# A vision and text block on one Trainium2 core: the expert down projection in split halves by columns, with its weights multiplied in by GpSimd

## The chip, the core and the metric

The kernel runs on one core of a Trainium2 chip. Its engines are TensorE (PE in the profile, with its weight loads as PEld), VectorE (DVE), ScalarE (ACT), GpSimd (POOL) and SyncE (SP); each has its own instruction queue, and they meet through semaphores. The metric is the time of one launch on the device, in microseconds.

## The reference

32 images become 196 patch rows each, a class row is put ahead and 128 text rows behind, so each of the 32 batch elements is a matrix of 325 tokens x 192. On it run one causal attention block (12 heads of 16) and one feed-forward block, each behind a layer norm and with a residual. The part that changes is the feed-forward block:

```python
shared_out = _expert(x, shared_gate, shared_up, shared_down)      # silu(x@gate) * (x@up) @ down, 192 -> 384 -> 192
routing_probs = sigmoid(x @ router_w + routing_bias)              # 3 experts
scores, indices = top_k(routing_probs, 2)
scores = scores / scores.sum(axis=-1, keepdims=True)
combine_w = (one_hot(indices, E) * scores[..., None]).sum(axis=-2)
h = silu(einsum('bsh,ehi->ebsi', x, routed_gate)) * einsum('bsh,ehi->ebsi', x, routed_up)
out_e = einsum('ebsi,eih->ebsh', h, routed_down)
return shared_out + einsum('ebsh,bse->bsh', out_e, combine_w)
```

All is float32. Where speed matters the kernel writes a number as a high part rounded to float32r (a format in which TensorE takes one pass) and a low part, the rest, and multiplies high by high, high by low and low by high.

## The kernel before

The program is a software pipeline over the batch elements, one **turn** per element, 32 in all; each engine runs `turn(i, at, N, D, T, L, A, F)`. In turn i the feed-forward part is that of element b3 = i - 1, scores, softmax and values those of b2 = i, and the first norm and the q, k, v projections those of b1 = i + 1. N is the number of patch tiles embedded in the turn: 2 in 12 turns, 1 in 16, 0 in the last four. A and L say whether there still is an element b2 or b1. A token matrix has three tiles of 128, 128 and 70 columns, so `COLS` is 326.

A turn has two halves on TensorE. In the **unit half** it alternates twelve `unit(k)` (gate and up products of 128 of the 4 x 384 inner columns, three units an expert, the shared one first) with twelve `score(k)`. ACT makes `tanh` of each unit and `exp` of each score, DVE makes the activation `ht[:, k]` of it (`gate`, `up`), and GpSimd multiplies the exponentials by the causal mask: `mask_last` and `mask_full` for each of the six head pairs p, behind exponentials 2p + 1 and 2p + 2. In the **second half** come `value(g)` for three groups of two pairs, each behind the masks of its pairs, then transpositions, projections, the second norm, the query and key transpositions, the router, and between them the down projections.

```python
def value(g, b, F):
    ...
    pe.wait_ge(masked.sem, masked.at(b, 4 * g + 4))
```

`down(e, t, b)` has the tokens of tile t as the stationary operand and `w_down_s` as the moving one, in plain float32, so its result lies by token rows. There is one accumulation for each of four experts and three tiles, of three products each: 36 products of 192 columns a turn. DVE's `sum_up(n)` adds them into `o` one expert at a time, the routed ones scaled by the routing weight of the row. That weight (`route[:, 6]`) is made by `route_turn` on TensorE (three 128 x 128 transpositions of `route_e`), `route_sum` and `route_pick` on DVE, in the second half of the turn.

GpSimd also makes the inverse root of each norm (`inverse_root`, four small instructions one behind the other). The first norm's comes behind the masks of pair 1, and ACT needs it ahead of its first `scaled` instruction, which stands behind exponential 6 (k = 6 of its loop, counted from 0). The order on each engine is the order of the code. SP's queue issues in a turn: the copy `residual<-h`, four loads of the next element, the doublings of q and k (each `DMA` of `double_q` and `double_k`), the store of embedded rows, and the two stores of `out`. Of these the doublings for element i are issued while TensorE is already in the unit half of turn i.

## Time and profile before

| | |
|---|---|
| three runs | 1615.01, 1617.93, 1619.52 us; median 1617.93 |
| span of the profiled execution | 1613.5 us (no other time of that execution is given) |
| PE / PEld busy | 98% / 91% of the span |
| DVE / ACT / POOL busy | 73% / 55% / 25% |
| mean granted TensorE clock | 0.995 |

Busy shares are averages over unlike stretches. A turn without a stall at its ends can be followed in the timeline: the turn that the rows below are taken from begins its unit 0 at 911.60 us and the next one at 960.19 us.

### The profile page before, as it was taken

To read this page: it belongs to the slowest core of one execution; us is meant where nothing else is said; L and a number is where in the kernel's file an instruction comes from. 1 tells how busy PE (TensorE), PEld (TensorE's weight loads), DVE (VectorE), ACT (ScalarE), POOL (GpSimd) and SP (SyncE) were. 2 spreads that over 40 slices of the span, in tenths; PEclk is the share of its full clock that TensorE was granted. 3 is DMA by queue.
4 is the path that set the end of the run, shared out by engine and by line. 5 is a ranking of instruction groups with operands and counts; after the bars stand their busy time and mean duration, and the time that the engine had idled before them with its cause. 6 is when DMAs were issued, how large, how long until landed. Compare 5 with 4: busy or idle time off the path is not lost.

```text
span 1613.5 us, 46379 instructions
## 1 busy us (share of the span) xinstructions
PE 1575.5 (98%) x16536; PEld 1471.0 (91%) x16536; DVE 1182.2 (73%) x3383; ACT 880.0 (55%) x1896; POOL 409.1 (25%) x647
## 2 busy tenths in 40 slices
PE   6899999999999999999999999999999999999999
PEld 6699999999999999999999999999999999998988
DVE  6776777767777777777677777677777677777665
ACT  4555554556545565545565555566555566555552
POOL 0332321232321323212323212323212323212320
PEclk8999999999999999999999999999999999999999
DMA  6211221111211112201111111111111111110110
GB/s 217 76 37 58 69 69 38 47 60 62 69 49 45 52 59 69 69 34 47 45 49 57 55 37 38 47 49 57 55 38 38 46 49 57 51 39 32 37 33 13
DMA packets 75382, 86.80 MB, mean 54 GB/s; under 512 B 12721, under 2 KB 64329, under 8 KB 75209
## 3 DMA queue, kind: packets, MB, share of 16 engines
q1 hardware_dynamic: 64776, 65.45, 11.9%
q10 hardware_dynamic: 10560, 20.74, 3.9%
q8 instruction: 29, 0.48, 0.1%
q14 instruction: 17, 0.13, 0.0%
HBM read 32.44 MB, written 12.51 MB: 28 GB/s over the span
## 4 chain that ended last, share of the span: by engine, by line
PE 86%; DVE 5%; DMA 5%; SPq 1%; issue 1%; ACT 1%; POOL 0%; DVEq 0%
PE ps L426 79%; PE ps L429 6%; DMA kt<-kt 5%; DVE kt L1174 1%; DVE o L1071 1%; PE ps L626 1%; DVE rotated L1162 1%; SPq L368 1%; DVE qk_split L1167 1%; DVE xt L1102 1%; DMA router_bias<-in_b_router 0%; DVE stats L1091 0%; ACT wf L809 0%; DVE rotated L1134 0%; DVE h L1195 0%
## 5 line engine op out<-in xcount | busy, mean ns | idle before, releaser
L426 PE MATMUL ps<-xt,wf 64*128 64x326 f32 x6912 | 593.0, 316 | 0.0
L426 PEld LDWEIGHTS ps<-xt,wf 64*128 64x128 f32 x6912 | 523.0, 186 | 11.3 <-ACT qt L809 5.8
L426 PE MATMUL ps<-w_down_s,ht 128*128 128x192 f32 (+1 forms) x2304 | 413.9, 329 | 0.0
L426 PEld LDWEIGHTS ps<-w_down_s,ht 128*128 128x128 f32 (+1 forms) x2304 | 350.9, 174 | 14.3 <-issue 0.2
L1048 DVE SCALAR_TENSOR_TENSOR gated<-tanh_g,ps 128x326 f32<-128x326 f32 x384 | 189.1, 492 | 198.9 <-ACT tanh_g L823 198.9
L816 ACT ACTIVATE rows<-h,rstd 128x192 f32<-128x192 f32 (+2 forms) x279 | 151.1, 564 | 211.4 <-POOL rstd L1018 206.6
L1007 POOL TENSOR_TENSOR probs<-probs,causal 128x512 f32<-128x512 f32 x192 | 228.7, 1191 | 131.8 <-ACT probs L834 131.8
L834 ACT ACTIVATE probs<-ps 128x792 f32<-128x792 f32 (+1 forms) x384 | 254.3, 663 | 13.6 <-PE ps L426 13.2
L823 ACT ACTIVATE tanh_g<-ps 128x326 f32<-128x326 f32 x384 | 170.1, 443 | 164.1 <-PE ps L426 162.6
L1001 POOL TENSOR_TENSOR probs<-probs,causal 69x140 f32<-69x140 f32 x192 | 89.0, 464 | 473.8 <-ACT probs L834 473.7
L1054 DVE TENSOR_TENSOR ht<-gated,ps 128x326 f32<-128x326 f32 x384 | 190.1, 495 | 13.1
L426 PE MATMUL ps<-wa_hi,xt 128*128 128x288 f32 (+3 forms) x576 | 161.3, 299 | 2.6 <-DVE xt L1102 2.6
L1012 POOL TENSOR_TENSOR rstd<-mean_var,power 128x3 f32<-128x3 f32 x64 | 12.4, 194 | 545.6 <-DVE mean_var L1096 545.6
L426 PE MATMUL ps<-qt,kt 64*128 64x326 f32 (+2 forms) x1152 | 121.3, 258 | 11.9 <-DMA kt<-kt 11.3
L809 ACT ACTIVATE xt<-ps 128x326 fp32r<-128x326 f32 x224 | 84.4, 440 | 77.7 <-PE ps L429 77.7
L426 PE MATMUL ps<-wb,xt 128*128 128x288 f32 (+3 forms) x576 | 119.4, 289 | 0.0
L426 PEld LDWEIGHTS ps<-qt,kt 64*128 64x128 f32 (+1 forms) x1152 | 91.8, 168 | 21.6 <-DMA kt<-kt 15.9
L426 PE MATMUL ps<-probs,v_ones 128*32 128x198 f32 (+2 forms) x2304 | 109.8, 333 | 1.3
L1071 DVE SCALAR_TENSOR_TENSOR o<-ps,route,o 128x192 f32<-128x192 f32 (+1 forms) x288 | 104.3, 407 | 8.7 <-PE ps L426 7.8
L426 PEld LDWEIGHTS ps<-wa_hi,xt 128*128 128x128 f32 (+1 forms) x576 | 101.4, 176 | 7.4 <-ACT xt L809 1.4
L426 PEld LDWEIGHTS ps<-probs,v_ones 128*32 128x32 f32 (+1 forms) x2304 | 68.1, 109 | 42.3 <-issue 5.9
L1102 DVE TENSOR_TENSOR xt<-ps,xt 128x326 fp32r<-128x326 f32 x224 | 100.8, 486 | 6.4 <-ACT xt L809 6.4
(105 smaller groups left out, 1917.5 us busy)
## 6 DMA issues: line engine op xcount, KB each, us to landing
kt<-kt SPq DMA_DIRECT2D x384, 40.8 KB, 1.8
x_s<-in_xp ACTq DMA_DIRECT2D x40, 384.0 KB, 3.1
qt<-qt SPq DMA_DIRECT2D x132, 81.5 KB, 1.9
residual<-h SPq DMA_DIRECT2D x31, 288.0 KB, 2.4
out<-o SPq DMA_DIRECT2D x32, 192.0 KB
qt<-qt ACTq DMA_DIRECT2D x60, 81.5 KB, 2.0
kept_rows<-embed_rows SPq DMA_DIRECT2D x44, 96.0 KB, 1.7
h<-kept_rows SPq DMA_DIRECT2D x30, 95.2 KB
```

Of the source, the lines that this page charges most:

```text
L426: return nc.tensor.matmul(dst, lhs, rhs, start=first, stop=last)
L429: return nc.tensor.transpose(dst, src, ident[0:n, 0:n])
L809: return nc.scalar.activation(dst, src, ACT.Copy)
L816: return nc.scalar.activation(dst, src, ACT.Identity, bias=coef[:, 3, t:t + 1], scale=coef[:, 0, t:t + 1])
L823: nc.scalar.activation(tanh_g[:, k % 2, :], ps[:, GATE[k % 3], 0:COLS], ACT.Tanh, scale=0.5).then_inc(tanh_done.sem, 1)
L834: nc.scalar.activation(dst, src, ACT.Exp, scale=ATTN_SCALE / ROOT_GAIN ** 2).then_inc(exp_done.sem, 1)
L1001: nc.gpsimd.tensor_tensor(d, d, shaped(causal[0:REAL2], [[0, 2], [1, COLS2]]), ALU.mult).then_inc(masked.sem, 1)
L1007: nc.gpsimd.tensor_tensor(d, d, shaped(causal[:], [[0, 2], [0, 2], [1, P]]), ALU.mult).then_inc(masked.sem, 1)
L1048: v.scalar_tensor_tensor(out=gated[:, k % 2, :], in0=tanh_g[:, k % 2, :], scalar=1.0, in1=ps[:, GATE[k % 3], 0:COLS], op0=ALU.add, op1=ALU ...
L1054: v.tensor_tensor(ht[:, k, :], gated[:, k % 2, :], ps[:, UP[k % 3], 0:COLS], ALU.mult).then_inc(h_ready.sem, 1)
L1071: last = v.scalar_tensor_tensor(out=o[0:c, t, :], in0=d, scalar=route[0:c, 6, t, e - 1:e], in1=o[0:c, t, :], op0=ALU.mult, op1=ALU.add)
L1102: v.tensor_tensor(dst, ps[:, bank, 0:COLS], f32(hi), ALU.subtract).then_inc(low.sem, 1)
```

## The change

The down projection is turned round. The weights become the stationary operand and the 326 token columns the moving one; both are split into high and low parts in float32r, and all four experts are summed in one PSUM accumulation. The routing weight, which was applied behind the product, must then be multiplied onto the activations ahead of it.

- **Products.** `down_main(units)` has three products of 326 columns for each of twelve units (output columns 0 to 127); `down_rest(units)` has two, since 64 output columns of the high and 64 of the low weights stand side by side. They are 60 products a turn, spread over the second half. `out_turn` makes six transpositions back to rows, and DVE's `sum_out` adds the result to `o`, which a DMA has filled with `h1`.
- **Routing.** `route_turn` is three small products instead of transpositions, behind unit 0; `route_sum` and `route_pick` follow on DVE behind `up(0)` and `up(1)`. SP stores the weights to DRAM (`kept_weights`, one element of 4 bytes at a time, 1152 of them) and loads them back spread over the partitions (`weight_cols`, 3 x 326 on each of 128).
- **Splitting.** GpSimd's `weigh(k)` multiplies the nine routed units; ACT's `round_h` copies each of twelve units to `h_high`; the low part is the difference, `low_h`: units 0 to 2 on DVE, 3 to 11 on GpSimd.
- **Moved.** The first norm's `inverse_root` goes from behind pair 1 to behind pair 2, its moments on DVE from behind unit 1 to behind unit 2. `norm1_turn` goes ahead of `y_to_rows`, and `y_to_cols` uses PSUM banks 6 and 7. ACT takes three `round_h` between `keep_y(1)` and `keep_y(2)`. The `out` stores of an element go to the next turn of SP, ahead of the new DMAs.
- **Storage.** `h_high` and `qk_split` lie under `probs`, `h_low` under `ht`, `w_down_lo` under the raw weights. In the last turn (A false) DVE makes all twelve low parts.

The core of the diff; its three `turn` functions are those of SP, GpSimd and TensorE (second half), in this order:

```diff
+            def store_out(b):
+                sp.wait_ge(summed.sem, summed.at(b, SUMS))
+                sp.dma_start(out[b, 0:2 * P, :].rearrange("(t p) d -> p t d", p=P), o[:, 0:2, :]).then_inc(stored.sem, 16)
+                sp.dma_start(out[b, 2 * P:TOKENS, :], o[0:REAL2, 2, :]).then_inc(stored.sem, 16)
+                sp.wait_ge(stored.sem, stored.at(b, 32))
+            def spread_weights(b):
+                sp.wait_ge(pick_chain.sem, pick_chain.at(b, 7))
+                sp.dma_start(weight_rows, route[:, 6].rearrange("p t e -> p (t e)"), allow_slow_non_contiguous=True).then_inc(weights_stored.sem, 16)
+                if later(b):
+                    sp.wait_ge(h_weighted.sem, h_weighted.at(b - 1, ROUTED))
+                sp.wait_ge(weights_stored.sem, weights_stored.at(b, 16))
+                sp.dma_start(weight_cols[:], weight_spread).then_inc(weights_loaded.sem, 16)
             def turn(i, at, N, D, T, L, A, F):
+                sp.wait_ge(h1_ready.sem, h1_ready.at(b3, 1))
+                if later(b3):
+                    store_out(b3 - 1)
+                sp.dma_start(o[:], h1[:]).then_inc(o_copied.sem, 16)
+                spread_weights(b3)
...
+            def down_main(units, b, A):
+                for k in units:
+                    wait_low(k, b, A)
+                    acc = ps[:, DOWN_BANK, 0:COLS]
+                    mm(acc, w_down_hi[:, k, :], h_low[:, k, :], k == 0, False)
+                    mm(acc, w_down_lo[:, k, :], h_high[:, k, :], False, False)
+                    last = mm(acc, w_down_hi[:, k, :], h_high[:, k, :], False, k == UNITS - 1)
+            def down_rest(units, b, A):
+                for k in units:
+                    wait_low(k, b, A)
+                    w = w_down_rest[:, k].rearrange("p s c -> p (s c)")
+                    mm(ps[:, DOWN_BANK + 1, 0:COLS], w, h_low[:, k, :], k == 0, False)
+                    last = mm(ps[:, DOWN_BANK + 1, 0:COLS], w, h_high[:, k, :], False, k == UNITS - 1)
...
+            def weigh(units, b):
+                for k in units:
+                    if k == CHUNKS:
+                        pool.wait_ge(weights_loaded.sem, weights_loaded.at(b, 16))
+                    pool.wait_ge(h_ready.sem, h_ready.at(b, k + 1))
+                    nc.gpsimd.tensor_tensor(ht[:, k, :], ht[:, k, :], weight_cols[:, k // CHUNKS - 1, :],
+                                            ALU.mult).then_inc(h_weighted.sem, 1)
             def turn(i, at, N, D, T, L, A, F):
                 for p in range(PAIRS):
                     if A:
                         mask_last(p, i)
                         mask_full(p, i)
-                    if L and p == 1:
+                    if L and p == 2:
                         inverse_root(i + 1, n1_moments, mean_var, rstd, n1_root, n1_ready)
+                    if p > 2:
+                        weigh(range(2 * p - 3, 2 * p - 1), i - 1)
+                weigh(range(2 * PAIRS - 3, UNITS), i - 1)
                 if A:
+                    for k in range(CHUNKS, UNITS):
+                        low_h(k, i - 1)
                     inverse_root(i, n2_moments, mean_var2, rstd2, n2_root, n2_ready)
...
             def turn(i, at, N, D, T, L, A, F):
                 if A:
                     for g in range(GROUPS):
                         value(g, b2, F)
+                if L:
+                    norm1_turn(b1, F)
                 if A:
-                    route_turn(b3)
-                    down(0, 0, b3)
                     y_to_rows(b2)
-                    if L:
-                        norm1_turn(b1, F)
-                    down(0, 1, b3)
...
+                down_main(range(0, 1), b3, A)
                 if L:
                     for t in range(TILES):
                         project_qkv(t, b1, A)
+                    pe.wait_ge(v_kept.sem, v_kept.at(b1, 1))
                 if A:
                     y_to_cols(b2, F)
+                down_main(range(1, 5), b3, A)
...
                     project_y(b2)
+                if N:
+                    embed(at, N)
+                down_main(range(5, 9), b3, A)
+                down_rest(range(0, 6), b3, A)
                 if A:
                     norm2_turn(b2)
+                down_main(range(9, UNITS), b3, A)
+                down_rest(range(6, UNITS), b3, A)
                 if L:
                     first_groups(b1)
                     for n in range(2, 2 * GROUPS):
                         qk_turn(n, b1, at, N)
+                out_turn(b3)
```

GpSimd in the unit half of a turn, from the third head pair on, before the change (`probs` rows are the masks, a pair of them for each head pair):

```order
L1001 TENSOR_TENSOR probs<-probs,causal 69x2x70
L1005 REGISTER_ALU
L1007 TENSOR_TENSOR probs<-probs,causal 128x2x2x128
L999 REGISTER_ALU
L1001 TENSOR_TENSOR probs<-probs,causal 69x2x70
L1005 REGISTER_ALU
L1007 TENSOR_TENSOR probs<-probs,causal 128x2x2x128
```

The same place after it, from the mask of the fourth head pair on, with what each instruction waits for:

```order
L1066 TENSOR_TENSOR probs<-probs,causal 69x2x70 [waits exp_done]
L1070 REGISTER_ALU
L1072 TENSOR_TENSOR probs<-probs,causal 128x2x2x128 [waits exp_done]
L1089 ISA
L1090 ISA [waits weights_loaded]
L1091 TENSOR_TENSOR ht<-ht,weight_cols 128x326 [waits h_ready]
L1090 REGISTER_ALU
L1091 TENSOR_TENSOR ht<-ht,weight_cols 128x326 [waits h_ready]
L1064 REGISTER_ALU
L1066 TENSOR_TENSOR probs<-probs,causal 69x2x70 [waits exp_done]
```

Two multiplications now stand between each two of the last pairs' masks, and the first of them waits for the loaded routing weights.

SP's queue at the end of a turn and the start of the next before the change:

```order
L348 DMA kept_rows<-embed_rows 128x192 [waits rows_added]
L398 DMA out<-o 128x2x192 [waits summed]
L400 DMA out<-o 69x192 [waits summed]
L307 UNCONDITIONAL_BRANCH
L307 ISA
L386 ISA [waits h1_ready]
L387 ISA [waits hidden_loaded]
L388 DMA residual<-h 128x576 [waits txt_loaded]
```

And after it, the start of a turn:

```order
L406 ISA [waits h1_ready]
L407 ISA [waits summed]
L407 DMA out<-o 128x2x192
L408 ISA
L408 DMA out<-o 69x192
L409 ISA
L425 DMA o<-h 128x576 [waits stored]
L413 ISA
L414 DMA kept_weights<-route 128x9x1 [waits pick_chain]
L416 ISA
L417 ISA [waits h_weighted]
L418 DMA weight_cols<-kept_weights 128x3x326 [waits weights_stored]
```

Behind the stores of `out` the queue now waits until they have landed, then copies `h1`, and only then sends the routing weights out and back.

## Rows read from the trace of the kernel before

**Rows 1.** The page, busy time by engine.
```profile
PE 1575.5 (98%) x16536; PEld 1471.0 (91%) x16536; DVE 1182.2 (73%) x3383; ACT 880.0 (55%) x1896; POOL 409.1 (25%) x647
```
**Rows 2.** Busy time in windows: from, to, width; PE, PEld, DVE, ACT, POOL; clock.
```profile
911.60:933.60 22.00, 21.20 (x304) 19.89 (x305) 14.21 (x35) 15.53 (x33) 11.24 (x16) 1.00 0.21 70
933.60:960.20 26.60, 26.60 (x212) 24.88 (x212) 21.84 (x71) 11.83 (x27) 1.47 (x4) 1.00 0.08 28
```
**Rows 3.** Timeline of TensorE in one turn: start, length, line, names, count.
```profile
911.60 1.62 PE L426 MATMUL ps<-xt,wf 64*128 64x326 f32 x18
913.98 0.45 PE L426 MATMUL ps<-qt,kt 64*128 64x326 f32 x4 [0.75 <-DMA kt<-kt]
...
931.31 3.48 PE L426 MATMUL ps<-probs,v_ones 128*32 128x326 f32 x72
...
939.63 0.37 PE L426 MATMUL ps<-wa_hi,xt 128*128 128x288 f32 x1
...
943.68 0.73 PE L429 MATMUL ps<-ident,y_wide 128*128 128x128 f32 x6
...
950.71 3.09 PE L426 MATMUL ps<-w_down_s,ht 128*128 128x192 f32 x18
953.64 1.00 PE L429 MATMUL ps<-ident,rows 128*128 128x128 f32 x9
```
**Rows 4.** Timeline of GpSimd in the same turn.
```profile
921.04 0.19 POOL L1012 TENSOR_TENSOR rstd<-mean_var,power 128x3 f32<-128x3 f32 x1
921.32 0.85 POOL L1014 TENSOR_TENSOR rstd<-rstd,power 128x3 f32<-128x3 f32 x1
...
922.52 0.20 POOL L1018 TENSOR_TENSOR rstd<-rstd,power 128x3 f32<-128x3 f32 x1
...
923.09 1.19 POOL L1007 TENSOR_TENSOR probs<-probs,causal 128x512 f32<-128x512 f32 x1
924.79 0.47 POOL L1001 TENSOR_TENSOR probs<-probs,causal 69x140 f32<-69x140 f32 x1 [0.51 <-ACT probs L834]
```
**Rows 5.** Timeline of ACT in the same turn.
```profile
924.60 0.55 ACT L816 ACTIVATE rows<-h,rstd 128x192 f32<-128x192 f32 x1
```
**Rows 6.** Timeline of SP's queue in the same turn: start and length of each issue.
```profile
919.15 0.59 SPq L369 DMA_DIRECT2D kt<-kt  x1
920.03 0.38 SPq L348 DMA_DIRECT2D kept_rows<-embed_rows  x1
920.70 0.42 SPq L398 DMA_DIRECT2D out<-o  x1
921.38 0.26 SPq L400 DMA_DIRECT2D out<-o  x1
```
**Rows 7.** Waits of SP's queue in the whole span: in all, times, longest.
```profile
SPq L98 <- DMA out<-o: 1.9, 1, 1.9
```
**Rows 8.** The page, DMA issues: KB each, median us from issue to landing.
```profile
x_s<-in_xp ACTq DMA_DIRECT2D x40, 384.0 KB, 3.1
...
residual<-h SPq DMA_DIRECT2D x31, 288.0 KB, 2.4
...
kept_rows<-embed_rows SPq DMA_DIRECT2D x44, 96.0 KB, 1.7
```
**Rows 9.** The page, DMA queue of SP: packets, MB, share of 16 engines' span.
```profile
q1 hardware_dynamic: 64776, 65.45, 11.9%
```
**Rows 10.** Timeline of all engines near the start, 66 to 77 us.
```profile
65.97 2.46 POOL L1014 TENSOR_TENSOR rstd<-rstd,power 128x3 f32<-128x3 f32 x1
65.98 2.62 DVE L1319 TENSOR_TENSOR wf<-ht,wf 128x1536 fp32r<-128x1536 f32 x2
...
70.38 1.85 PE L429 MATMUL ps<-ident,rows 128*128 128x128 f32 x9 [1.63 <-ACT rows L816]
```
**Rows 11.** Two windows behind that stall, columns as in Rows 2.
```profile
72.00:74.00 2.00, 1.17 (x9) 0.91 (x9) 1.49 (x4) 2.00 (x6) 0.00 (x0) 0.50 0.39 128
...
76.00:78.00 2.00, 2.00 (x18) 1.96 (x16) 0.57 (x1) 0.31 (x1) 0.00 (x0) 0.55 0.29 100
```

More of the change, by code:

```diff
@@ L100, in sb, with under @@
             return ctx.enter_context(nc.sbuf_tensor(name, shape, dt))
+        def under(name, shape, *others):
+            with nc.sbuf_tensor(name, shape, F32) as first:
+                pass
+            return first, *(sb(other, like, dt) for other, like, dt in others)
         def signal(name, per_batch):
@@ L659, in route_turn, with wait_low @@
                 last.then_inc(route_turned.sem, 1)
-            def down(e, t, b, L=True, A=True):
-                if t == 0 and e == 0:
-                    pe.wait_ge(h_ready.sem, h_ready.at(b, UNITS if A else UNITS - 2))
-                    if not later(b):
-                        pe.wait_ge(s_halve, 2)
-                for c in range(CHUNKS):
-                    last = mm(accumulator(e, t, L, A), ht[:, CHUNKS * e + c, tile_cols(t)], w_down_s[:, CHUNKS * e + c, :],
-                              c == 0, c == CHUNKS - 1)
-                if t:
-                    last.then_inc(down_done.sem, 1)
+            def wait_low(k, b, A):
+                if k < CHUNKS:
+                    pe.wait_ge(shared_low.sem, shared_low.at(b, k + 1))
+                else:
+                    pe.wait_ge(routed_low.sem, routed_low.at(b, k - CHUNKS + 1))
@@ new lines, in down_main @@
+            def down_main(units, b, A):
+                for k in units:
+                    if k == 0 and not later(b):
+                        pe.wait_ge(s_down_low, 2)
+                    wait_low(k, b, A)
[3 more added lines that the diff above has]
+                    last = mm(acc, w_down_hi[:, k, :], h_high[:, k, :], False, k == UNITS - 1)
+                    if k == UNITS - 1:
+                        last.then_inc(down_done.sem, 1)
@@ L862, in turn @@
                 if A:
-                    for g in range(GROUPS):
-                        act.wait_ge(value_done.sem, value_done.at(b2, g + 1))
-                        copy(y_cols[:, g, :], ps[:, VALUE_BANK[g], 0:COLS]).then_inc(y_kept.sem, 1)
+                    keep_y(0, b2)
+                    keep_y(1, b2)
+                    round_h(range(0, CHUNKS), b3)
+                    keep_y(2, b2)
                 if L:
@@ L868, in turn @@
                         keep_high(h, xt[:, 2 * h, :], XT_BANK + h, n1_turned, b1, xt_hi)
+                round_h(range(CHUNKS if A else 0, EARLY_HIGH), b3)
+                if L:
                     for t in range(TILES):
@@ L1249, in turn @@
                         moments(h0, stats, stats_chain, b1, rstd, mean_var, n1_moments)
-                if F:
-                    route_sum(b3)
-                    for n in range(3):
-                        route_pick(n, b3)
-                if A:
-                    divide_rows(b2)
+                for k in range(CHUNKS if A else UNITS):
+                    low_h(k, b3)
                 if L:
@@ L1283, in turn @@
                         rms_step(n, b1)
-                if F:
-                    for n in range(2, 4):
-                        sum_up(n, b3)
                 if N:
@@ L1306, in turn @@
                     keep_k(2, b1, KEEP_BANK)
[L1307 to L1313 removed]
+                elif A:
+                    for j in range(BLOCKS):
+                        norm2_low(j, b2)
             def split_ffn(j):
```

253 lines of the change are left out of this document (130 added, 123 removed).

## The prediction

> **What bounds the kernel now.** I read first the page's busy shares: TensorE is busy 98% of the span [rows 1], far ahead of the others. Then the windows of one turn [rows 2]: in its second half TensorE has no idle time, in its unit half 0.80 us of 22, and that is one wait, 0.75 us ahead of score 0 for the doubling of k [rows 3]. So work taken off TensorE is time saved, unless it has to wait for something new. DVE is busy 14.2 of 22 and 21.8 of 26.6 us, ACT less, GpSimd nearly only in the unit half (11.2 of 22). The reader should see that the second half is where GpSimd is free, and that the unit half is where it is not.
>
> I count a turn's time t from the start of its unit 0, at 911.60 [rows 3]. `value(0)` starts at 931.31, and the three groups take 3.48, so `value(2)`, which needs the masks of all six pairs, starts at 931.31 + 2.32, that is t = 22.0.
>
> **TensorE's own work.** Removed are 36 products in plain float32, each of two records: 18 records take 953.64 - 950.71 = 2.93 us [rows 3], 0.163 each, 72 of them 11.7 us a turn. Added are 60 of float32r with 326 columns. The nearest rows are the 30 products of 288 columns from 939.63 to 943.68 [rows 3]: 0.135 each, in proportion 0.153, so 9.1 us. Its bounds are 60 x 0.135 = 8.1 and 60 x 0.163 = 9.8. Six transpositions to rows are added, 0.65 us by the six of `y_wide` (0.73 with their end, 0.57 to the next instruction) [rows 3]. Routing has three instructions before and after, taken as equal. Together 9.1 + 0.65 - 11.7 = -2.0 us a turn (bounds -3.0 and -1.2).
>
> **GpSimd's new work.** No row has `weigh` or `low_h`. A mask of 512 elements takes 1.19, one of 140 takes 0.47 [rows 4]; the line through them gives 0.83 us for 326, and the two masks are its bounds (0.47 and 1.19). The Trainium skill, GPSIMD Engine Reference, section 3.1, has 4497 ns for a two-input addition of 2048 elements, which by elements alone would be an estimate of 0.72 us here. Four of the nine `weigh` stand between masks, so from the fourth pair on each pair costs 2 x 0.83 + 0.47 + 1.19 = 3.3 us; TensorE gives it (931.31 - 913.98)/6, or 2.9 us, a pair. GpSimd thus falls behind there even if nothing else is late. The other five and nine `low_h`, 11.6 us, lie in the half where it was free; their users come late (the first routed unit behind all of `project_qkv`), so I cost them at nothing. Without that cover each would be 0.83.
>
> The first norm's root takes 922.72 - 921.04 = 1.7 us [rows 4]. Behind pair 2's mask, which ends at 923.09 + 1.19 = 924.28, it ends at 926.0; ACT now starts the instruction that needs it at 924.60 [rows 5]. ACT stands 1.3 us, with the tanh and exp of unit 7 behind it, and score 8 waits for that exponential: some 0.4 us of it is ACT's own lead, 0.9 reaches TensorE.
>
> **The wait that I think decides: the routing weights.** The first `weigh` waits for `weights_loaded`, and behind it in GpSimd's queue stand the masks of pairs 4 and 5, for which `value(2)` waits. The weights go through SP's queue, and there they are behind the doublings (last issued at 919.15), the store of rows (920.03) and both stores of `out`, the second issued at 921.38 [rows 6], t = 9.8. DVE has long made them by then, in the shadow of units 0 and 1. What follows is new and goes one behind the other:
> - SP waits until `out` has landed: 1.9 us in the one row that shows it [rows 7], t = 11.7.
> - The copy `o<-h` and the start of the next issue, 0.6 us (issues take 0.26 to 0.60) [rows 6]: 12.3.
> - The store of 1152 single elements, 72 on each of 16 DMA engines. The least is the 1.7 us of a store of rows [rows 8]. The most is 72 packets more at the mean time of a packet of this queue, 0.119 x 16 x 1613.5/64776 = 47 ns [rows 9], or 1.7 + 3.4 = 5.1. Small elements should be cheaper than the mean packet of 1 KB, but nothing here shows it, so I take the middle, 3.4: 15.7.
> - A handover (0.1) and the load of 489 KB. 288 KB take 2.4, 384 KB 3.1 [rows 8], on that line 489 KB 3.9; the bounds are 2.4 and 3.9, I take 3.5 as it is nearer the larger. In 28 turns ACT's loads of `x_s`, 384 KB each, start shortly before and could add up to 3.1.
>
> So the weights are there at t = 12.3 + 3.4 + 0.1 + 3.5 = 19.3 (bounds 16.5 and 21.4, with `x_s` ahead 24.5). Then come two `weigh`, pair 4, two `weigh`, pair 5: 2 x 3.3 = 6.6 us, and `value(2)` starts at 25.9 instead of 22.0. That is a stall of **3.9 us**. If the weights were early, GpSimd's own lag remains: it would reach the first `weigh` after mask 3 at t = 16.9 (exponential 7 is 0.9 to 1.3 late), finish at 23.5 and leave a stall of 1.5. The 0.9 us at score 8 is part of either number, since it moves TensorE towards the late masks.
>
> **What is hidden or small.** The 0.75 us ahead of score 0 stays: the same doublings are issued as late, and TensorE has nearly the same work between `first_groups` and score 0 (0.98 of `down` goes, 0.65 of transpositions and the routing products come). ACT gains 12 `round_h` and a copy, some 6 us in 48, behind work that the 3.9 us stall holds up anyway. The key transpositions have no `down(3, 2)` between them any more, so the copy of q shows: +0.2. DVE loses twelve `sum_up` and gains four sums and three low parts. Unit 1 waits for `sum_out`, but router, unit 0, routing and score 0 lie between.
>
> **Sum.** -2.0 + 0.2 + 3.9 = +2.1 us in each of the 31 turns that have value groups, 65 us. The last turn and the two ends: +3 (two splits in place of one halving at the start; a copy, six transpositions and four sums behind the last product, where one sum was). The profiled span is 1613.5; the median of the runs lies 4.4 above it. 1613.5 + 65 + 3 + 4.4 = 1686, I say 1685.
>
> **Against two rules.** In the start-up GpSimd's power instruction takes 2.46 us instead of 0.85 while two DVE instructions run whose both inputs are in SBUF [rows 4, 10]. So it can be held up for the length of DVE's. In the second half DVE has some ten such instructions per turn against 14 of GpSimd's. If each of ten waited half of 0.83 us, that is 4 us, which DVE's 4.8 us of idle time there [rows 2] covers; if each waited the whole, 8.3 us, three of them would show: +5.6 us a turn in all. The Trainium skill, SBUF — State Buffer, "Practical consequences", says that such a pair shares one read port under a lock held for the whole instruction; by that rule, the trace agrees, the sum would lie between my +2.1 and that +5.6.
>
> A stall can also cost clock. After a wait of 1.63 us and transpositions [rows 10] the granted clock was 0.50, which is 1.2 GHz, and it was 0.55 in the window that ends six microseconds later [rows 11]. Here a longer wait in `value`, then transpositions, comes every turn; at half clock for 5 us each turn loses another 2.5. The Trainium skill, TensorE: Matmul & The Clock Gate, "HAM oscillation", tells of repeated idle gaps that throw the clock back each time. Against it speaks that 0.75 us of idle per turn leave the clock at 1.00 [rows 2].
>
> **Rivals.**
> - *Weights late, clock kept* (my forecast), 0.40: 1640 to 1720.
> - *Weights late and the clock falls, or GpSimd and DVE hold each other up*, 0.27: +4.6 a turn, 31 x 4.6 + 3 + 1617.9 = 1764; 1720 to 1800.
> - *Weights in time.* If the small store costs little more than one of rows and the load 2.4 us, they are there at 16.5. With 1.5 us of stall the turn changes by -0.3, in all 1612, no difference. With `weigh` nearer 0.7 us the mask chain ends with score 8's 0.9 alone: -0.9 a turn, 1593; without that, -1.8, 1565. It turns at a stall of 1.8 us, weights at t = 17.2. For it speaks that elements of 4 bytes may go far faster than 47 ns. 0.33, of which 0.20 for faster, 0.08 no change, 0.05 slightly slower.
> - *The product is not cheaper*: if float32r of 326 columns cost 0.163, TensorE saves only 1.2 and the forecast is 25 us longer; within the first case's range.
>
> **Numbers.** A measurement of this kernel tells some 0.3% (5 us) from no change. The range from 1590 to 1770 leaves out the fastest tenth (below 1590 both the load and GpSimd would have to be at their lower ends) and a tenth above. The forecast's own range is 1640 to 1720. Faster 0.20, same 0.08, slower 0.72.
>
> **What would show it.** In the trace after: 60 products at 0.15 us; the load of `weight_cols` landing at t = 17 to 22; GpSimd waiting at its first `weigh` for a DMA; TensorE waiting 3 us ahead of the third value group for GpSimd's `probs`; 0.9 us at score 8. The prediction is wrong if GpSimd does not wait for the DMA, if the small store lands in 2 us, or if the large new wait stands elsewhere, as in DVE's chain to `first_groups`.

## The result and the profile after

The changed kernel takes **2071.8 us** (median of 4 runs, 2069.3 to 2074.2) against 1617.6 before: 1.281 times, 95% interval 1.279 to 1.282. The direction was forecast, the size was not: it is 302 us above the upper end of the range.

The page of the kernel after, its busy time, SP's and ACT's DMA queues and the chain that ended last:

```profile
PE 1632.0 (79%) x16440; PEld 1494.8 (72%) x16440; DVE 1215.3 (59%) x3233; ACT 1035.5 (50%) x2314; POOL 865.5 (42%) x1214
...
q1 hardware_dynamic: 119704, 91.06, 13.9%
q10 hardware_dynamic: 10560, 20.74, 10.8%
...
PE 29%; DMA 27%; SPq 17%; POOL 12%; issue 7%; ACT 4%; DVE 3%; POOLq 1%; ACTq 0%; DVEq 0%
```

TensorE went from 98% [rows 1] to 79%, and more than half of the chain is now DMAs, SP's queue and GpSimd. The windows of one turn show where in a turn (columns as in [rows 2]; its unit 0 begins at 1104.28, the next one at 1167.60):

```profile
1104.28:1126.00 21.72, 20.83 (x280) 19.84 (x281) 14.93 (x46) 14.09 (x29) 8.00 (x12) 1.00 0.49 74
1126.00:1139.40 13.40, 2.50 (x26) 1.33 (x25) 2.31 (x5) 3.02 (x8) 6.24 (x9) 0.58 0.22 52
1139.40:1146.00 6.60, 6.57 (x47) 5.48 (x48) 2.08 (x6) 2.78 (x7) 5.87 (x8) 0.55 0.00 0
1146.00:1167.50 21.50, 20.94 (x156) 19.45 (x154) 17.37 (x46) 11.94 (x29) 6.98 (x11) 1.00 0.10 34
```

The unit half is nearly as it was. Then come 13.4 us in which TensorE works 2.5, and 6.6 us in which it works all the time at a granted clock of 0.55, near 1.2 GHz. TensorE's timeline of this turn, against [rows 3]:

```profile
1104.28 1.62 PE L465 MATMUL ps<-xt,wf 64*128 64x326 f32 x18
...
1119.51 0.45 PE L465 MATMUL ps<-qt,kt 64*128 64x326 f32 x4 [0.60 <-ACT probs L877]
...
1127.65 0.22 PE L465 MATMUL ps<-probs,v_ones 69*32 69x70 f32 x1 [1.95 <-issue]
1128.19 2.28 PE L465 MATMUL ps<-probs,v_ones 69*32 69x70 f32 x25 [0.31 <-issue]
1139.43 2.21 PE L465 MATMUL ps<-probs,v_ones 128*32 128x326 f32 x24 [8.96 <-POOL probs L1072]
...
1149.36 0.73 PE L468 MATMUL ps<-ident,y_wide 128*128 128x128 f32 x6
...
1156.44 0.31 PE L465 MATMUL ps<-h_high,w_down_lo 128*128 128x326 f32 x1
1156.59 0.31 PE L465 MATMUL ps<-h_high,w_down_hi 128*128 128x326 f32 x1
...
1159.07 1.61 PE L468 MATMUL ps<-ident,rows 128*128 128x128 f32 x9
```

`value(2)` starts 35.15 us after unit 0, where it was 22.0. It waits 8.96 us for GpSimd's mask; over the span this wait is 331.8 us in 31 turns, 10.7 a turn. GpSimd's timeline (against [rows 4]) and SP's queue (against [rows 6]) say why:

```profile
1119.53 1.20 POOL L1072 TENSOR_TENSOR probs<-probs,causal 128x512 f32<-128x512 f32 x1 [0.96 <-ACT probs L877]
1133.16 1.59 POOL L1091 TENSOR_TENSOR ht<-ht,weight_cols 128x326 f32<-128x326 f32 x2 [12.42 <-DMA weight_cols<-kept_weights]
...
1138.12 1.17 POOL L1072 TENSOR_TENSOR probs<-probs,causal 128x512 f32<-128x512 f32 x1
1139.25 3.87 POOL L1091 TENSOR_TENSOR ht<-ht,weight_cols 128x326 f32<-128x326 f32 x5
```

```profile
1114.06 0.26 SPq L408 DMA_DIRECT2D out<-o  x1
1116.40 0.50 SPq L425 DMA_DIRECT2D o<-h  x1
1117.04 0.51 SPq L414 DMA_DIRECT2D kept_weights<-route  x1
1128.69 0.38 SPq L418 DMA_DIRECT2D weight_cols<-kept_weights  x1
```

SP issues the small store 12.76 us into the turn (forecast 12.3). The load that waits for it is issued 11.65 us later (over the 32 turns 9.4 to 12.3, median 11.2); the forecast gave that store 3.4 us and at most 5.1. The weights are used 28.9 us into the turn, not 19.3.

To compare kernels I take the exponential of the router, which ACT makes once a turn: 31 of them, so 30 turns between the first and the last. In the kernel before, after, and the last version of this study:

```profile
L906 ACT ACTIVATE route_e<-ps,router_bias x31: 508/512/531, 124.4 to 1582.0; 4x326 f32<-4x326 f32 x31
```

```profile
L969 ACT ACTIVATE route_e<-ps,router_bias x31: 508/511/526, 141.2 to 2029.2; 4x326 f32<-4x326 f32 x31
```

```profile
L982 ACT ACTIVATE route_e<-ps,router_bias x31: 507/510/526, 127.0 to 1569.8; 4x326 f32<-4x326 f32 x31
```

That is 48.59, 62.93 and 48.09 us a turn, so the mean loss is 14.34. The turn shown is 63.32 us long, 14.7 more than 48.59: +13.15 up to `value(2)` (35.15 for 22.0) and +1.6 behind it (28.17 for 26.57). Behind it stand:
- +2.4 of slow clock: from `value(2)` to the transpositions of `y_wide` 9.93 us, and 7.54 in the last version, whose TensorE has the same products there at full clock;
- +0.6 at the second norm's transpositions, which stretch to 1.61 for 1.00 because ACT's rows come late;
- -1.3 of products, where the forecast had -2.0: the 60 products take 9.5 us (in the last version, at full clock), the six transpositions 0.6, and the seven groups of `down` before took 11.5;
- +0.1 at the key transpositions, and -0.4 for the router's, which have moved into the unit half.

These add up to +1.4; the other 0.2 I have not traced.

### The profile page after: what moved, and what is told of

Read it like the earlier page. It is cut to its first block, busy times and chain, and to the rows that moved or that the text cites. A ratio compares the mean times of both kernels' runs of the same rounds, so it can differ in the third digit from the quotient of the medians.

```text
span 2069.0 us, 47646 instructions
## 1 busy us (share of the span) xinstructions
PE 1632.0 (79%) x16440; PEld 1494.8 (72%) x16440; DVE 1215.3 (59%) x3233; ACT 1035.5 (50%) x2314; POOL 865.5 (42%) x1214
## 4 chain that ended last, share of the span: by engine, by line
PE 29%; DMA 27%; SPq 17%; POOL 12%; issue 7%; ACT 4%; DVE 3%; POOLq 1%; ACTq 0%; DVEq 0%
PE ps L465 23%; DMA kept_weights<-route 16%; DMA weight_cols<-kept_weights 7%; PE ps L468 6%; SPq L392 5%; SPq L391 5%; POOL probs L1072 3%; DMA out<-o 3%; SPq L386 3%; POOL h_low L1097 3%; POOL ht L1091 3%; ACT rows L859 2%; POOL probs L1066 1%; DVE kt L1258 1%; SPq L371 1%
## 5 line engine op out<-in xcount | busy, mean ns | idle before, releaser
L465 PEld LDWEIGHTS ps<-xt,wf 64*128 64x128 f32 x6912 | 553.3, 186 | 13.5 <-ACT qt L852 10.1
L465 PE MATMUL ps<-probs,v_ones 128*32 128x326 f32 (+2 forms) x2304 | 163.3, 405 | 367.2 <-POOL probs L1072 331.8
L1091 POOL TENSOR_TENSOR ht<-ht,weight_cols 128x326 f32<-128x326 f32 x288 | 223.8, 804 | 410.6 <-DMA weight_cols<-kept_weights 410.6
L1097 POOL TENSOR_TENSOR h_low<-ht,h_high 128x326 fp32r<-128x326 f32 x279 | 238.8, 889 | 140.5 <-ACT h_high L852 140.5
L852 ACT ACTIVATE y_cols<-ps 128x326 f32<-128x326 f32 x96 | 41.0, 443 | 382.9 <-PE ps L465 360.8
L465 PE MATMUL ps<-qt,kt 64*128 64x326 f32 (+2 forms) x1152 | 164.6, 269 | 18.0 <-ACT probs L877 18.0
L852 ACT ACTIVATE h_high<-ht 128x326 fp32r<-128x326 f32 x384 | 151.8, 482 | 6.8 <-POOL ht L1091 6.8
L465 PE MATMUL ps<-h_low,w_down_hi 128*128 128x326 f32 x384 | 134.9, 351 | 4.4 <-DVE h_low L1157 4.4
L465 PE MATMUL ps<-h_high,w_down_lo 128*128 128x326 f32 x384 | 121.5, 316 | 0.0
L465 PE MATMUL ps<-h_high,w_down_hi 128*128 128x326 f32 x384 | 121.0, 315 | 0.0
```

What stands on the lines that cost most here:

```text
L465: return nc.tensor.matmul(dst, lhs, rhs, start=first, stop=last)
L852: return nc.scalar.activation(dst, src, ACT.Copy)
L1091: nc.gpsimd.tensor_tensor(ht[:, k, :], ht[:, k, :], weight_cols[:, k // CHUNKS - 1, :], ALU.mult).then_inc(h_weighted.sem, 1)
L1097: nc.gpsimd.tensor_tensor(h_low[:, k, :], ht[:, k, :], f32(h_high[:, k, :]), ALU.subtract).then_inc(routed_low.sem, 1)
```

## The experiments

Three theories stood at the start. **Theory 1**: 1152 single elements take long to store, so the weights are late and the masks behind them. **Theory 2**: the round trip through DRAM, or its collision with other transfers, costs that whatever the number of elements. **Theory 3**: GpSimd and DVE hold each other up, or the clock falls for its own reasons. "Per turn" below is from the router's exponential. All numbers are medians; the kernel before took 1617 to 1618 beside each.

**128 runs instead of 1152 elements.** The same elements are stored as runs of 36 B, which puts the weights in a wrong order; the load is as it was.

```diff
-        weight_rows = kept_weights.rearrange("e (t p) -> p (e t)", p=P)
+        weight_rows = bass.AP(kept_weights.tensor, kept_weights.offset, [[EXPERTS * TILES, P], [1, EXPERTS * TILES]])
```

> The routing weights are stored as 128 runs of 36 bytes instead of 1152 single elements, and loaded as before; they arrive in the wrong order, so the output is not the reference's. Theory 1 (the single elements cost the time, some 0.13 us for each of the 72 that fall to a DMA engine): from the issue of the store to the issue of the load at most 3 us instead of 11.6, TensorE waits 3 to 5 us a turn ahead of the third value group instead of 13, the clock recovers for the most part, and the time is about 1700 us (1660 to 1760). Theory 2 (the round trip through DRAM or the collision with the loads of x_s costs it, whatever the number of elements): still 9 us or more between the two issues and over 2000 us. Theory 3 (GpSimd and DVE hold each other up, and the clock falls for reasons of its own): at most half of the 454 us comes back, over 1840 us.

Measured 1784.2 us, 1.105 [1.101, 1.109]. Between the issue of the store and that of the load, SP's queue shows 1.9 us where there were 11.65:

```profile
1022.69 0.50 SPq L414 DMA_DIRECT2D kept_weights<-route  x1
1024.62 0.38 SPq L418 DMA_DIRECT2D weight_cols<-kept_weights  x1
```

So 288 of the 454 us hang on the number of elements. Theory 2 falls, and so does theory 3 as it stood, which had at most half of the 454 come back. But the time is above the range of theory 1.

**No weights at all.** GpSimd multiplies by ones, without store, load or wait (the routing weights are left out).

```diff
-                spread_weights(b3)
...
-                    if k == CHUNKS:
-                        pool.wait_ge(weights_loaded.sem, weights_loaded.at(b, 16))
...
-                    nc.gpsimd.tensor_tensor(ht[:, k, :], ht[:, k, :], weight_cols[:, k // CHUNKS - 1, :],
+                    nc.gpsimd.tensor_tensor(ht[:, k, :], ht[:, k, :], ones_cols[:],
```

> The routing weights are left out: no store, no load, and GpSimd multiplies by ones, at once. All other work stays. Theory 1: only 0.6 us at score 8 and up to 1 us of GpSimd's own lag remain, against 2 us less work on TensorE: 1570 to 1615 us. Theory 3: GpSimd's and DVE's contention and a lowered clock stay, over 1700 us.

Measured 1878.2 us, 1.161 [1.159, 1.163]: far outside, and 94 us *slower* than with the 128 runs and their late weights. This miss opened the second half of the study. The rows of DVE, GpSimd and TensorE behind the last mask:

```profile
1023.37 3.90 POOL L1089 TENSOR_TENSOR ht<-ht,ones_cols 128x326 f32<-128x326 f32 x5
...
1024.05 7.71 DVE L1156 TENSOR_TENSOR h_low<-ht,h_high 128x326 fp32r<-128x326 f32 x3 [1.61 <-ACT h_high L852]
1027.23 3.35 POOL L1095 TENSOR_TENSOR h_low<-ht,h_high 128x326 fp32r<-128x326 f32 x4
...
1031.00 0.64 PE L465 MATMUL ps<-h_low,w_down_hi 128*128 128x326 f32 x1 [4.47 <-DVE h_low L1156]
```

```profile
1031.00:1036.40 5.40, 4.87 (x19) 4.49 (x20) 3.25 (x9) 0.91 (x3) 0.00 (x0) 0.52 0.00 0
1036.40:1040.00 3.60, 3.60 (x30) 3.60 (x29) 2.51 (x7) 2.79 (x9) 0.00 (x0) 1.00 0.00 0
```

DVE's three low halves should take 1.5 us. They take 7.7: the first alone takes 6.9 and ends just behind nine GpSimd instructions that run from 1023.37 to 1030.58 without a gap, the other two take 0.49 each. TensorE waits 4.47 us for the first of them, and the 5.4 us of projections behind that wait run at a clock of 0.52. Over the whole span this group is the costliest of DVE, 2380 ns in the mean for one, against 518 in the changed kernel itself, where GpSimd stands waiting for the weights while DVE makes them:

```profile
L1156 DVE TENSOR_TENSOR h_low<-ht,h_high 128x326 fp32r<-128x326 f32 x105 | 244.3, 2380 | 49.9 <-ACT h_high L852 49.9
```

```profile
L1157 DVE TENSOR_TENSOR h_low<-ht,h_high 128x326 fp32r<-128x326 f32 x105 | 49.0, 518 | 67.0 <-ACT h_high L852 67.0
```

**Store and load kept, GpSimd doesn't wait.** Ones as above, with `spread_weights` left in.

> Store and load of the weights stay as they are, but GpSimd multiplies by ones and does not wait for them. Theory 1 (only the wait costs): within 10 us of the kernel without store and load. Theory 2 in a second form (the traffic of 1152 small packets delays other transfers: x_s, the doublings, the loads of h): 30 us or more above it.

Measured 1769.6 us, 1.095 [1.092, 1.099]. GpSimd's wait alone is worth 302 us against the changed kernel. Both forecasts had 1868 or more and both missed: with store and load kept the kernel is 109 us faster than without them. In it DVE's low halves take 899 ns in the mean, where the kernel without weights had 2380. One more thing is seen, of which the kernel after has the same (this is its ACT):

```profile
1128.26 0.44 ACT L866 ACTIVATE tanh_g<-ps 128x326 f32<-128x326 f32 x1 [3.76 <-remote]
```

ACT stands still until the small store is through (the load is issued at 1128.69), and the profile finds no signal on the core for it. Such "remote" waits of ACT (72 to 113 us in all) and "issue" waits of TensorE (35 to 69) are in the three kernels of this study that store 1152 single elements, and in no other. In the kernel after they lie ahead of GpSimd's late masks, which would hold TensorE anyway. Why DVE gets through in this kernel, though GpSimd runs nine instructions in a row here too (1026.79 to 1035.14), is not shown.

**Masks first.** GpSimd makes all masks, then all nine multiplications.

```diff
-                    if p > 2:
-                        weigh(range(2 * p - 3, 2 * p - 1), i - 1)
-                weigh(range(2 * PAIRS - 3, UNITS), i - 1)
+                weigh(range(CHUNKS, UNITS), i - 1)
```

> GpSimd makes all masks of a turn first and then all nine multiplications; the weights come as late as before. Theory 1: the third value group starts in time, and the wait moves to the second piece of the down projection, which needs the low part of unit 3, about t = 37 against 30: some 7 us a turn instead of 13, 1800 to 1920 us. If the order on GpSimd were the whole cause, the time would be under 1650 us; if it did not matter, 2070.

Measured 1908.4 us, 1.180 [1.177, 1.183], in the range of theory 1. TensorE's wait for masks is nearly gone (10.5 us in the whole span, 331.8 in the changed kernel), but the late weights still reach it: 47.1 us in 49 waits for GpSimd's low halves, and remote waits of 113.4. The masks' place behind the weights is worth 163 of the 454 us; the other 291 stay with the masks first.

**Theory 4** came out of the kernel without weights: a DVE instruction with both inputs in SBUF does not get through while GpSimd runs two-input instructions back to back. The test adds one wait to the kernel without weights.

```diff
+                pool.wait_ge(shared_low.sem, shared_low.at(i - 1, CHUNKS))
                 weigh(range(2 * PAIRS - 3, UNITS), i - 1)
```

> The kernel without weights (ones, no store, no load; 1878.2 us) with one wait more: GpSimd waits for VectorE's three low halves (units 0 to 2) before its last five multiplications. Output is not the reference's, since the routing weights are left out. Theory 4 (new): a VectorE subtraction with two SBUF inputs doesn't get through while GpSimd runs two-input instructions back to back. Its record of 6.9 us lies over GpSimd's nine instructions, TensorE waits 4.5 us for it in each turn (140.7 us in 33 waits) and then runs some 5 us of projections at half clock (2.6 us more). With the wait the three take 0.5 us each: 1878 minus 31 x 4.5 to 7.1 is 1739 to 1658; I expect 1665. Theory 1 (only the late weights cost) says nothing of it, and a rival that VectorE is late for a reason of its own (its input from ScalarE, its own program) leaves 1878 or more, since GpSimd starts its last nine instructions 1.6 us later.

(The wait stands ahead of the last three multiplications, units 9 to 11; the expectations say five.) Measured 1667.3 us, 1.031 [1.029, 1.032], forecast 1665: a wait more, 211 us less. Of the 6.8 us a turn, 4.5 are TensorE's wait; the other 2.3 I put down to the clock, 0.989 in the mean for 0.934.

**The whole computation with weights in time.** DVE transposes the nine weights of each token in blocks of 32 x 32, SP stores them as 36 runs of 128 B in four transfers, behind the doublings of pair 4, and loads them behind those of pair 5.

```diff
-                sp.dma_start(weight_rows, route[:, 6].rearrange("p t e -> p (t e)"), allow_slow_non_contiguous=True).then_inc(weights_stored.sem, 16)
+                for q in range(4):
+                    sp.dma_start(weight_rows[:, q], w_turned[32 * q:32 * q + EXPERTS * TILES, :]).then_inc(weights_stored.sem, 16)
...
+                elif n == 7:
+                    last = v.transpose(w_turned[:], w_pad[:])
...
+                    if spread is not None and m == STORE_AFTER:
+                        store_weights(spread)
+                    if spread is not None and m == STORE_AFTER + 1:
+                        load_weights(spread)
```

> The whole computation, with the weights transposed by VectorE (32 x 32 blocks), stored in four transfers of nine runs of 128 B, behind the doublings of pair 4, and loaded behind those of pair 5. Theory 1 alone (element-wise store, late weights): the wait for the weights is gone, and 2072 falls to 1640 (1620 to 1700). Theory 4 (VectorE held off by GpSimd) with theory 1: the weights' wait is gone, but GpSimd then runs its multiplications as in the kernel without weights, and VectorE's low halves are held off as there: 1878 (1840 to 1900), slower than the run-wise store with its late weights (1784). Theory 2 (a round trip costs the same whatever the number of elements): 1950 or more.

Measured 1871.4 us, 1.158 [1.156, 1.160], as theory 4 said and not as theory 1 did. GpSimd waits for the load once, at the start. The new wait of TensorE is the one of the kernel without weights:

```profile
PE ps L478 <- DVE h_low L1170: 136.0, 32, 4.6
```

**The same, with GpSimd's wait** for the three low halves:

> The one before (transposed, four stores of runs, early store and load) and GpSimd's wait for VectorE's three low halves before its last five multiplications. The whole computation. Theories 1 and 4 together: as the kernel without weights with that wait, 1670 (1640 to 1740), some 200 under the one before. Theory 1 alone: no difference to the one before, or 30 to 50 us more, since GpSimd gets a wait.

Measured 1661.5 us, 1.028 [1.026, 1.030]. DVE's low halves fall from 2305 to 702 ns:

```profile
L1171 DVE TENSOR_TENSOR h_low<-ht,h_high 128x326 fp32r<-128x326 f32 x105 | 68.0, 702 | 50.0 <-ACT h_high L865 50.0
```

The time is in the range of theories 1 and 4 together.

**And the first norm as before the change** (root behind pair 1, moments behind unit 1):

> As the one before, with the first norm's root of GpSimd back behind pair 1 and its moments behind unit 1, as in the kernel before the change. This takes the root (1.7 us of GpSimd) away from ahead of pair 3's masks, for which TensorE waits 0.6 us at score 8: 20 to 30 us less than the one before, 1645 (1610 to 1720). If it ends below 1610, this version beats both kernels.

Measured 1654.8 us, 1.024 [1.022, 1.026], 6.7 us less, a third of the least that I expected. TensorE's wait for the exponential went, but one for DVE took its place (the second row), since the moments now stand ahead of unit 2's product. The first row was there before, with 32.4 us:

```profile
PE ps L478 <- DVE xt L1200: 32.5, 33, 1.3
...
PE ps L478 <- DVE ht L1152: 19.0, 30, 0.7
```

**Two small moves against these two waits**: moments back behind unit 2, root left behind pair 1; DVE's low parts of the attention rows ahead of its third rotation.

```diff
                     rms_sum(0, b1)
-                    rotate(2, b1)
                 if A:
                     for h in range(2):
                         keep_low(h, xt[:, 2 * h + 1, :], xt[:, 2 * h, :], YT_BANK + h, yt_hi, b2, yt_lo)
+                if L:
+                    rotate(2, b1)
```

> The whole computation: transposed weights, four stores of runs, early store and load, GpSimd's wait for the three low halves, the first norm's root behind pair 1 as in the kernel before, its moments behind unit 2 as in the change, and VectorE's low parts of the attention's rows ahead of the third rotation. The version at 1654.8 us shows TensorE waiting 0.65 us a turn at unit 5 for VectorE's product (seven route steps and the moments stand before it) and 0.96 us at the attention's projection for VectorE's low parts (the rotations before them take 0.9 to 1.0 us each instead of 0.36 while GpSimd runs its low halves). Theory 4: both waits are VectorE's order and go: 1655 minus 31 x 1.6 is 1605 (1590 to 1635), under the kernel before (1618). Rival: the waits only move to the next thing that VectorE makes (moments of the second norm, key halves): 1645 to 1660.

Measured 1650.4 us, 1.022 [1.020, 1.025]: the rival, and by the times alone no clear gain, since the five runs (1650.1 to 1659.1) overlap those of the version before (1652.4 to 1659.0). Both waits fell (32.5 to 12.5 us, and 19.0 to none), and a third appeared, for the second norm's rows:

```profile
960.77 1.61 PE L481 MATMUL ps<-ident,rows 128*128 128x128 f32 x9 [1.32 <-ACT rows L872]
```

**The store turned and nothing else**, at its late place, and **the same with GpSimd's wait**:

> The changed kernel with only the store changed: VectorE transposes the weights (32 x 32 blocks), and four transfers of nine runs of 128 B store them where the one of 1152 single elements did. The whole computation. Theory 1: store and load take some 2 and 4 us, weights at t 20 to 21 instead of 28.9, GpSimd's multiplications behind it as in the version with 128 runs of 36 B: 1775 (1740 to 1810). Theory 2 (the number of elements doesn't matter): 2072. Theory 4 adds that VectorE's low halves are held off here too, mean over 1.5 us of one.

> The one before (turned weights, store and load at their late place) with GpSimd's wait for VectorE's three low halves before its last five multiplications. Theory 4: low halves back at 0.5 us each; but the multiplications come later by what GpSimd waits, so that the value products and the down products are late by the weights alone: 1720 (1680 to 1760). Without contention as a cause: as the one before.

Measured 1809.8 [1.117, 1.122] and 1808.7 us [1.118, 1.122]. The first is at the edge of its range, the second a miss. In both TensorE waits for late masks (125.3 and 124.5 us in 31 waits), GpSimd being held at the weights as before. The low halves are slow here too (2166 and 1755 ns), but they are made while TensorE waits anyway. So GpSimd's wait did not bring them to 0.5 us here, as theory 4 had forecast: DVE starts them while GpSimd runs the late masks and the multiplications between them, all ahead of the place of the wait. TensorE's row, from the first of the two:

```profile
1043.45 2.21 PE L468 MATMUL ps<-probs,v_ones 128*32 128x326 f32 x24 [3.70 <-POOL probs L1075]
```

The two causes cover each other: cure one, and the other takes over. With the weights in time and no wait, TensorE waits for the low halves (1871); with the store cheap but late, it waits for the masks (1810).

**384 runs of three elements**, weights again in a wrong order:

> The changed kernel with the same 1152 elements stored as 384 runs of three (12 B), which leaves the weights in the wrong order in DRAM and so changes the output; load and waits as they are. Theory 1 with a price per run: between 128 runs (2.0 us) and 1152 (10.0 to 11.6 us) a straight line gives 8.3 ns a run, 4.1 us for 384 and some 1820 us in all (1790 to 1870). With a price per element or byte instead the store keeps its 10 us and the time 2072.

Measured 1865.7 us, 1.154 [1.151, 1.157], inside the range. The page's row of the store, whose last number is the median from issue to landing (it is 2.0 with 128 runs):

```profile
kept_weights<-route SPq DMA_DIRECT2D x32, 4.5 KB, 4.4
```

The straight line of the expectation had 4.1 us. From 128 to 384 runs the price is 9.4 ns a run ((4.4 - 2.0)/256). For 1152 elements the page gives no landing; by the median from issue to issue, 11.2 us, it is 8.9 from 384 to 1152 ((11.2 - 4.4)/768). It goes by the run and not by the byte, at some 9 ns a run.

**DVE's order.** The version with the two moves, and behind them the residual addition and the second norm's moments ahead of the third rotation and the steps:

```diff
-                    rotate(2, b1)
                     rms_sum(1, b1)
-                    rms_sum(2, b1)
-                    for n in range(2):
-                        rms_step(n, b1)
                 if A:
                     add_residual(b2)
                     dve.wait_ge(h1_ready.sem, h1_ready.at(b2, 1))
                     moments(h1, stats2, stats2_chain, b2, rstd2, mean_var2, n2_moments)
                 if L:
-                    for n in range(2, RSQRT_STEPS):
+                    rotate(2, b1)
+                    rms_sum(2, b1)
+                    for n in range(RSQRT_STEPS):
```

> The version at 1650.4 us with VectorE's third rotation and the sums and steps behind it put behind the residual addition and the second norm's moments. In that version the wait at the attention's projection had fallen to 0.3 us and a wait of 1.32 us for the second norm's rows had come in its place: VectorE began the residual addition 2.3 us after TensorE had made its last product, behind two SBUF instructions of 0.8 to 0.9 us each (0.36 free). Theory 4 with VectorE's order: the addition starts as TensorE ends, GpSimd's root some 2 us earlier, the wait of 1.3 us is gone and nothing else takes its place: 1650 minus 31 x 1.3 is 1610 (1595 to 1630), at or just under the kernel before (1617). Rival: the key halves are now late (VectorE has the same work in the same time), so the transpositions wait some 1 us: 1635 to 1655, and what is left of the loss is VectorE's time under GpSimd's traffic, wherever it is put.

Measured **1606.9 us**, 0.9932 [0.9918, 0.9945], forecast 1610: the whole computation, and 11 us under the kernel before. That is 0.7%: clear of the noise (1605.9 to 1607.6 against 1616.0 to 1619.3), and small. Its two halves of a turn, columns as in [rows 2] (the second window runs 0.24 us into the next turn):

```profile
955.47:977.35 21.88, 21.84 (x310) 20.60 (x314) 16.12 (x49) 15.82 (x34) 14.34 (x21) 1.00 0.32 105
977.35:1003.10 25.75, 24.97 (x203) 23.21 (x205) 21.86 (x53) 16.44 (x40) 13.35 (x18) 1.00 0.10 32
```

TensorE's rows of the value groups and of the next transpositions, which the comparison of the clock above used (`value(2)` begins two thirds into the first, at 977.35):

```profile
975.03 3.48 PE L478 MATMUL ps<-probs,v_ones 128*32 128x326 f32 x72
...
984.89 0.73 PE L481 MATMUL ps<-ident,y_wide 128*128 128x128 f32 x6
```

The addition now waits for TensorE instead of coming 2.3 us late, and the steps behind it take 0.20 to 0.23 us; GpSimd has finished its low halves by then (at 991.54):

```profile
989.23 0.56 DVE L1294 TENSOR_TENSOR h<-ps,residual 128x384 f32<-128x384 f32 x1 [1.13 <-PE ps L478]
...
992.66 0.20 DVE L1240 TENSOR_SCALAR rms<-rms 128x72 int32<-128x72 int32 x1
992.89 0.23 DVE L1242 TENSOR_TENSOR rms<-rms 128x72 f32<-128x72 f32 x1
```

In the changed kernel the same two stand under GpSimd's low halves, ahead of the addition:

```profile
1152.65 0.90 DVE L1226 TENSOR_SCALAR rms<-rms 128x72 int32<-128x72 int32 x1
1153.59 0.84 DVE L1228 TENSOR_TENSOR rms<-rms 128x72 f32<-128x72 f32 x1
```

## Why the prediction was wrong

**The mechanism was the forecast one**: weights behind `out` in SP's queue, GpSimd standing at its first `weigh` with the masks of pairs 4 and 5 behind it, TensorE waiting at the third value group. The point that failed is the term "The store of 1152 single elements": 3.4 us, with 5.1 as its most. It measured 11.65 in the turn shown, 11.2 in the median, and with it the weights came 9.6 us later than forecast (8.2 of the store, 0.9 of load and handover, 0.5 ahead of it). The upper bound was no bound: I took the mean time of a packet of that queue, 47 ns [rows 9], and argued that a small element is cheaper. The runs show some 9 ns a run over all. If the 1152 lie evenly on 16 engines, that is some 145 ns for each on its engine, three times the mean packet of 1 KB. Collision with `x_s` was at most a small part: in the last four turns, which have no such load, 10.0 to 11.3 us pass.

**The clock** was a rival (+2.5 a turn); it was measured at 2.4, together with late weights. The rival's time, 1764, is missed all the same, since the store had the same size in it. The 8.96 us were not what brought the clock down in the turn shown: it is 1.00 up to 1128.20, 0.53 in the 0.8 us behind that and 0.50 from 1129.00 to 1145.00, so it fell behind the two "issue" waits of 1.95 and 0.31 us and stayed low through the long one. The Trainium skill, TensorE: Matmul & The Clock Gate, "HAM oscillation", speaks of repeated gaps that bring the clock down; the trace agrees, 0.896 in the mean against 0.995 before.

**GpSimd against DVE.** In the changed kernel I find only the 0.6 us at the second norm, since the late weights keep GpSimd out of DVE's way (low halves of 518 ns). So "DVE's 4.8 us of idle time covers it" was nearly right for that kernel, and wrong for the case behind it. The rival *weights in time* (1565 to 1612) is refuted: with the weights in time the kernel takes 1871, since nine of GpSimd's instructions hold one of DVE's, on the path, for 6.9 us. I had bounded the price by one instruction of GpSimd for each of DVE's. The Trainium skill, SBUF — State Buffer, "Practical consequences", says that a DVE instruction with two SBUF inputs contends with a GpSimd instruction that reads SBUF, since its second input comes through a read interface that the two share. The runs agree in kind and show more in size, since a whole row of instructions kept DVE out.

**TensorE's own work** was forecast at -2.0 and is -1.3, near its bound of -1.2. The products do take 0.15 us each within a group (1156.44 to 1156.59), but the first of a group takes 0.23 to 0.28 up to the next one (1155.25 to 1155.53), so all 60 take 9.5 us and not 9.1; and the 72 records taken away were worth 11.5 us, not 11.7. The 0.75 us ahead of score 0 did not stay either: TensorE waited 11.3 us in 18 turns for the doubling of k before, and never after.

**Right in size**: `weigh` 0.78 and `low_h` 0.85 for 0.83; 6.3 us from the landing of the weights to `value(2)` for 6.6; 0.60 at score 8 for 0.9; the second `out` issue at 9.8. At the key transpositions TensorE waits 0.46 us, but from their start to the next product's they and it take only 0.1 more than before (2.08 us for 1.98), for 0.2 forecast.

**Where the gain of -2.0 went.** The last version has it partly: 48.09 a turn for 48.59. Of the 2.0, 0.7 was never there (above), and the new waits that remain are 0.46 (q's copy) and 0.30 (projection). That gives -0.5, as measured; the smaller terms are left out, so the agreement can be chance. Its start and end are 7 us longer than before, for 3 forecast.

**Open.** What holds ACT and TensorE ("remote", "issue") during the element-wise store: it comes and goes with that store, but its mechanism was not tested. And when DVE gets between two GpSimd instructions, which theory 4 does not say: in the kernel without weights it did not in nine; in the one that keeps store and load its three low halves passed in 2.89 us, and the kernel is 109 us faster; in the one with 128 runs DVE's three passed in 5.80 us while GpSimd's five stretched from 3.90 to 4.65; and in the version at 1661.5 us DVE's rotations each passed beside GpSimd's low halves in 0.9 to 1.0 us for 0.36.

## What to carry to other kernels

Count the runs of a transfer, not its bytes: bound a store of single elements by a row that has such elements, and if there is none, leave the upper end wide open. When one engine is held up, ask what that wait keeps apart; a cure that brings the work forward can cost more than the delay, as the weights did here, and a wait added at the right place can pay for itself many times (210 us here, in two kernels). After such a cure read the chain of the next engine anew: four waits came up one behind the other, and only the last order gave the gain.

## What the runs showed of the hardware

- A store from SBUF to DRAM of 4.5 KB in all takes 2.0 us in 128 runs and 4.4 in 384; in 1152 runs 11.2 pass from its issue to that of the load that waits for it (9.4 to 12.3). That is some 9 ns a run.
- While the store of 1152 elements is under way, ACT stood up to 5.4 us and TensorE up to 4.0 us, and the profile names no signal on the core that they waited for.
- A DVE subtraction of 128 x 326 with both inputs in SBUF takes 0.49 us alone and took 6.9 us beside nine GpSimd instructions in a row. DVE's instructions with one input in PSUM kept their time beside GpSimd's: `up` 0.50 beside its multiplications, the residual addition 0.55 beside its low halves (0.56 without).
- After a wait of TensorE of 4.5 us (in the kernel without weights) the granted clock was 0.52 for 5.4 us of nearly dense work and then 1.00. In the kernel after it had fallen behind waits of 1.95 and 0.31 us, and was 0.55 in the 6.6 us behind the one of 8.96.
